# Attention layer of a graph network: maxima stored feature-major, only denominators turned back, another order on TensorE, the maximum's column copied by ScalarE

## The chip, the cores and the metric

One core of one Trainium2 chip runs the whole kernel. The metric is the time of one execution on the device in microseconds (us), the median of several runs. The profile is one execution taken by the hardware profiler. PE is TensorE, with PEld its weight loads; DVE is VectorE; ACT is ScalarE; POOL is GpSimd; SP is SyncE, which here only issues transfers.

## The reference, cut to what matters

Four graph layers follow one another on 6250 nodes and 200,000 edges sorted by destination, each with a residual and a layer norm. The change is in the fourth, an attention layer with 4 heads of 16 features:

```
xl = (x @ W_l + b_l);  xr = (x @ W_r + b_r);  e = edge_attr @ W_e       # 16 edge features
g = leaky_relu(xl[src] + xr[dst] + e, 0.2)
logits = einsum('ehc,hc->eh', g, att)
amax   = segment_max(logits, dst);   ex = exp(logits - amax[dst])
denom  = segment_sum(ex, dst);       alpha = ex / (denom[dst] + 1e-16)
out    = segment_sum(xl[src] * alpha, dst) + bias
out    = batch_norm(out) * gamma + beta;   return gelu(out + x)
```

Sums and maxima by destination are made over sorted edges: a running scan is restarted wherever the destination changes, and the row at a node's last edge is its result.

## The kernel before, in words

The edges are cut into two halves of 100,000. 512 edges of either half make a group, so there are 196 groups (n = 0 to 195, the last of 160 edges). On chip a tile is feature-major: 128 partitions are 2 halves x 64 features, and 512 columns are edges in order. The fourth layer is `edges_4`, followed by `finish_4`. The third, `edges_3`, has the same form with other steps and is not touched.

Each engine runs its own program, and semaphores join them. `each_group` takes for an engine a list of (lag, step) and runs for every tick t each step on group t - lag, in the order of the list. That written order is all that sets the order of work on an engine; nothing is reordered. The body is unrolled four times.

The steps of `edges_4` for one group:

- POOL `gather`: 8 indirect transfers fetch xl[src] into `got` (4 buffers), L1681. A buffer is free when PE has turned it (`turned_got`).
- SP `load`: 7 transfers, the destination rows (`first`), the edge features (`ea`), the marks (`mk`) and resets (`rs`), L1654 to L1657; it waits for `resets` and `owned` of four groups earlier.
- PE `gathered_rows`: turns `got` into `p_got` in four pieces; ACT `their_rows` copies that to `theirs`, L1751.
- PE `edge_inputs`: turns `first` into `p_first` and `ea` into `p_small`; ACT `edge_rows` copies the latter to `eat`, L1746.
- DVE `spread`: a scan hands each destination's row on to its edges, `own`, L1836.
- PE `add_edge_terms`: two matmuls add `eat` and `theirs` into `p_pre`, L1717 and L1719. DVE `attend` adds `own`, L1844; ACT `fifths` and DVE `leak` make the leaky relu `act_in`, L1757 and L1850.
- PE `score`: the logits into `p_logit`, L1733, then the spread resets into `p_reset`, L1735. ACT `keep_logits`, L1789.
- DVE `maximum`: copies the last column of the other `top` into column 0 of this one, L1814, then scans the maxima, L1818.
- DVE `exponents`: L1824, L1825, L1828; ACT `exps`: exp of both, L1762 and L1765, and the maxima, masked to one row of each head, into `p_reset`, L1766.
- DVE `accumulate`: scan of denominators `den`, L1858; weights times `theirs`, L1861; `mixed`, which puts denominators and maxima of a head in different rows of one tile, L1864; scan of the sums `run`, L1869.
- PE `turn_back` and `small_back`: turn `run` and `mixed` into edge-major `p_out` and `p_small` in four pieces each. ACT `to_rows` copies them to `rows`, L1772 and L1777, and `store` sends those to `t3` in DRAM, 72 columns for each edge: 64 sums, 4 denominators, 4 maxima.

The lags and the orders before are:

```
PE:  (1, gathered_rows), (0, edge_inputs), (1, add_edge_terms), (3, turn_back), (3, small_back), (1, score)
ACT: (1, their_rows), (0, edge_rows), (2, exps), (1, fifths), (3, to_rows), (3, store), (1, keep_logits)
DVE: (2, maximum), (2, exponents), (1, attend), (0, spread), (1, leak), (2, accumulate)
```

In `score` the reset matmul waits for `mixes`, so for the DVE's L1864 of the group before. `finish_4` fetches for each node the row at its last edge with 49 indirect transfers (L973), reads the row where the first half ends (`carry`), and normalizes.

Of the kernel before, what the change touches and what calls it, by code (L numbers as in the profile page):

```python
# [17 lines left out]
I32 = mybir.dt.int32  # L18
# [50 lines left out]
class Group:  # L69


    def __init__(self, it, base, unroll=UNROLL):
        self.it, self.base, self.unroll = it, base, unroll
        self.n = base if it is None else it * unroll + base
        self.row = self.n * W
        self.w = TAIL if it is None and base == NG else W
        self.p = self.w // C
        self.zero = it is None and base == 0
        self.late = it is None and base + LAG > NG
# [100 lines left out]
def build(nc, x, src, dst, ea16, ea64, ew, w0a, b0a, w0b, b0b, u1, w1a, b1a, w1b, b1b, g1, be1,  # L180
          w2a, b2a, w2b, b2b, w2g, b2g, wl, bl, wr, br, we, att, bias3, g3, be3, out):
    ctx = ExitStack()
    with ctx:
# [5 lines left out]
        t3 = dram("t3", [E, T3], F32)  # L189
        start2 = dram("start2", [E, D], F32)  # L190
# [50 lines left out]
        edges_4(nc, sb, ps, sem, ix4, ea16, marks, tabg[1], start3, prime, t3, ident, sel2, we, att)  # L241
        finish_4(nc, sb, ps, sem, X, order[0], t3, valid, bias3, g3, be3, out)
# [1365 lines left out]
def edges_4(nc, sb, ps, sem, ix, ea16, marks, tabg, start, prime, t3, ident, sel2, we, att):  # L1608
# [5 lines left out]
    with Stage(nc) as c:  # L1614
        WE, AT = sb(c, "WE", [2 * ED, P]), sb(c, "AT", [P, P])
        AV = sb(c, "AV", [P, 1])
        onesr, second = sb(c, "onesr", [P, R]), sb(c, "second", [P, R])
        for_top, for_den = sb(c, "for_top", [P, 1]), sb(c, "for_den", [P, 1])
# [5 lines left out]
        own, theirs, fifth, act_in, logit, expo, decay, run, den, mixed = (  # L1624
            [sb(c, f"{n}{i}", [P, W]) for i in range(2)] for n in ("own", "theirs", "fifth", "act_in", "logit", "expo", "decay", "run", "den", "mixed"))
# [8 lines left out]
        stored = [sem(c, f"stored{i}") for i in range(2)]  # L1634
        (resets, turned_first, turned_ea, turned_got, featured, gotten, summed_ea, owned, added, leaked, scored,
         logits, fifthed, carried, maxed, lefts, shifted, falls, grown, decayed, topped, weighted, summed, dens, mixes, rowed, smalls, drained, drained_small) = (
            sem(c, n) for n in ("resets", "turned_first", "turned_ea", "turned_got", "featured", "gotten", "summed_ea",
                                "owned", "added", "leaked", "scored", "logits", "fifthed", "carried", "maxed", "lefts", "shifted", "falls", "grown",
                                "decayed", "topped", "weighted", "summed", "dens", "mixes", "rowed", "smalls", "drained", "drained_small"))
        with nc.Block() as block:  # L1640
            @block.sync
            def _(sp):
# [16 lines left out]
                each_group(sp, (0, load))  # L1659

            @block.gpsimd
            def _(pool):
                nc.gpsimd.memset(onesr[:, :], 1.0).then_inc(made, 1)
                nc.gpsimd.memset(blocks[0][:, :], 1.0).then_inc(made, 1)
                pool.wait_ge(made, 2)

                nc.gpsimd.affine_select(out=second[:, :], in_=onesr[:, :], compare_op=ALU.is_equal, fill=0.0, base=-1,
                                        pattern=[[-HC, R]], channel_multiplier=1).then_inc(made, 1)
# [3 lines left out]
                pool.wait_ge(made, 4)  # L1672
# [15 lines left out]
            def _(pe):  # L1688
# [23 lines left out]
                def add_edge_terms(g):  # L1712
# [6 lines left out]
                    nc.tensor.matmul(p_pre[:, 0:g.w], ident[:, :], theirs[s][:, 0:g.w], start=False, stop=True).then_inc(summed_ea, 1)  # L1719

                def small_back(g):

                    pe.wait_ge(mixes, g.n + 1)
                    if not g.late:
                        pe.wait_ge(featured, g.n + LAG + 1)
                    else:
                        pe.wait_ge(drained_small, g.n)
                    turn_to_edges(nc, p_small[:, :].rearrange("p (c q) -> p c q", c=C), mixed[g.slot(2)], g, ident).then_inc(smalls, 1)

                def score(g):  # L1730
# [3 lines left out]
                    wait_from(pe, mixes, g.n)  # L1734
                    nc.tensor.matmul(p_reset[:, 0:g.w], sel2[:, :], rs[g.slot(AHEAD)][:, 0:g.w], start=True, stop=True).then_inc(resets, 1)  # L1735

                each_group(pe, (1, gathered_rows), (0, edge_inputs), (1, add_edge_terms), (3, turn_back), (3, small_back), (1, score))

            @block.scalar
            def _(act):  # L1740
                act.wait_ge(zeroed, 3)

# [5 lines left out]
                def their_rows(g):  # L1748
                    act.wait_ge(turned_got, g.n + 1)
                    wait_from(act, weighted, g.n - 1)  # L1750
                    nc.scalar.activation(by_place(theirs[g.slot(2)], g), by_block(p_got, g), ACT.Copy).then_inc(gotten, 1)  # L1751
# [7 lines left out]
                def exps(g):  # L1759
                    s = g.slot(2)  # L1760
                    act.wait_ge(shifted, g.n + 1)
                    nc.scalar.activation(p_logit[s][:, 0:g.w], p_logit[s][:, 0:g.w], ACT.Exp).then_inc(grown, 1)  # L1762
                    act.wait_ge(falls, g.n + 1)
                    wait_from(act, summed, g.n - 1)
                    nc.scalar.activation(decay[s][:, 0:g.w], expo[s][:, 0:g.w], ACT.Exp).then_inc(decayed, 1)  # L1765
                    nc.scalar.activation(p_reset[:, 0:g.w], top[s][:, 1:1 + g.w], ACT.Identity, scale=for_top[:, 0:1]).then_inc(topped, 1)  # L1766

                def to_rows(g):
# [7 lines left out]
                    for q in range(2):  # L1776
                        ins = nc.scalar.activation(rows[s][0:g.p, :, :, D + q * HEADS:D + (q + 1) * HEADS].rearrange("p h c f -> p c h f"),  # L1777
                                                   small[:, :, :, :, q], ACT.Copy)
                    ins.then_inc(drained_small, 1)
# [11 lines left out]
                each_group(act, (1, their_rows), (0, edge_rows), (2, exps), (1, fifths), (3, to_rows), (3, store), (1, keep_logits))  # L1791
# [4 lines left out]
            def _(dve):  # L1796
                nc.vector.memset(WE[:, :], 0.0).then_inc(zeroed, 1)
                dve.wait_ge(weights_in, 64)
                dve.wait_ge(made, 5)
                nc.vector.tensor_scalar(AT[:, :], blocks[2][:, :], AV[:, 0:1], None, ALU.mult).then_inc(zeroed, 1)  # L1800

                nc.vector.tensor_reduce(for_top[:, :], second[:, :], AX.X, ALU.add).then_inc(zeroed, 1)
                dve.wait_ge(zeroed, 3)
                nc.vector.tensor_scalar(for_den[:, :], for_top[:, :], -1.0, 1.0, ALU.mult, ALU.add).then_inc(zeroed, 1)
                dve.wait_ge(zeroed, 4)

                def maximum(g):
                    s = g.slot(2)
                    wait_from(dve, topped, g.n - 1)
                    if g.zero:  # L1810
                        nc.vector.memset(top[s][:, 0:1], NEG).then_inc(carried, 1)
                    else:
                        dve.wait_ge(maxed, g.n)
                        nc.vector.tensor_copy(top[s][:, 0:1], top[1 - s][:, W:W + 1]).then_inc(carried, 1)  # L1814
                    dve.wait_ge(carried, g.n + 1)
                    dve.wait_ge(logits, g.n + 1)
                    dve.wait_ge(resets, g.n + 1)
                    nc.vector.tensor_tensor_scan(top[s][:, 1:1 + g.w], p_reset[:, 0:g.w], logit[s][:, 0:g.w], top[s][:, 0:1], ALU.add, ALU.max).then_inc(maxed, 1)  # L1818

                def exponents(g):  # L1820
# [3 lines left out]
                    nc.vector.tensor_tensor(p_logit[s][:, 0:g.w], p_logit[s][:, 0:g.w], top[s][:, 1:1 + g.w], ALU.subtract).then_inc(shifted, 1)  # L1824
                    nc.vector.tensor_tensor(p_reset[:, 0:g.w], top[s][:, 0:g.w], p_reset[:, 0:g.w], ALU.add).then_inc(lefts, 1)  # L1825
# [26 lines left out]
                def accumulate(g):  # L1852
# [4 lines left out]
                    wait_from(dve, mixes, g.n - 1)  # L1857
# [3 lines left out]
                    nc.vector.tensor_tensor(p_logit[s][:, 0:g.w], theirs[s][:, 0:g.w], p_logit[s][:, 0:g.w], ALU.mult).then_inc(weighted, 1)  # L1861
                    dve.wait_ge(topped, g.n + 1)
                    wait_from(dve, smalls, g.n - 1)
# [164 lines left out]
```

## Time and profile before

| | |
|---|---|
| median of 3 runs | 5972.57 us (5963.78 to 5984.49) |
| the profiled execution, its own time | 5978.15 us |
| its span, first to last instruction | 5976.4 us |
| busy over the span | PE 65%, DVE 65%, POOL 59%, ACT 31% |
| gathers of `edges_3` issued | 1344.4 to 3303.6 us |
| gathers of `edges_4` issued | 3468.7 to 5756.5 us |
| first DVE instruction of `finish_4` | 5811.2 us |

The profile's own time is 0.1% above the median. A share over the whole span mixes stages with different limits, so the stage of `edges_4`, some 2340 us long, is to be read by itself.

### The profile page before, as it was taken

The page shows a single profiled execution, that of the slowest core. Times are in us where ns is not written, and L with a number is a line of the kernel's source. Part 1 is how long each engine was busy: PE and PEld are TensorE (multiplying, and loading weights), DVE is VectorE, ACT ScalarE, POOL GpSimd, SP SyncE. Part 2 cuts the span into 40 slices and gives each one's busy share as a digit, 9 for nine tenths or more (in the row PEclk, how much of TensorE's full clock was granted, in tenths as well). Part 3 has the DMA queues.
Part 4 walks back from the last instruction along what each step waited for, and adds up shares of the span by engine and source line. Part 5 has one row for each costly group of instructions (what it writes and reads, how often), then busy time and mean ns, then how long its engine had stood idle before and what let it go on. Part 6 is the DMA issues. An engine that isn't in the chain of part 4 may idle for free. (4 is left out here: it accounts for less than half of the span.)

```text
span 5976.4 us, 57806 instructions
## 1 busy us (share of the span) xinstructions
PE 3875.9 (65%) x12134; PEld 2170.3 (36%) x12134; DVE 3858.3 (65%) x4586; ACT 1848.3 (31%) x3478; POOL 3534.9 (59%) x3662
## 2 busy tenths in 40 slices
PE   3556669765555555555555358778877887777860
PEld 2334446432333333333333224444444444444430
DVE  9988887653333333333333457887788778888775
ACT  1233335461111111111111123443344334444330
POOL 5440025337777777777777676666666666666632
PEclk7666667776666666666666556665677666666665
DMA  8666569715444444444444234343344334334420
GB/s 188 218 190 203 177 168 272 120 35 127 116 118 118 118 118 119 118 119 118 119 118 107 52 76 88 87 87 83 84 88 88 83 85 86 87 86 88 85 58 21
DMA packets 1372199, 674.80 MB, mean 113 GB/s; under 512 B 1049375, under 2 KB 1252761, under 8 KB 1371141
## 3 DMA queue, kind: packets, MB, share of 16 engines
q1 hardware_dynamic: 1095862, 338.24, 24.3%
q0 software_dynamic: 116848, 124.33, 11.6%
q10 hardware_dynamic: 159390, 211.24, 10.1%
q14 instruction: 76, 0.61, 0.0%
q8 instruction: 23, 0.38, 0.0%
HBM read 344.06 MB, written 329.35 MB: 113 GB/s over the span
## 5 line engine op out<-in xcount | busy, mean ns | idle before, releaser
L1681 POOL DMA_INDIRECT got<-tabg,ix x1568 | 1479.7, 944 | 809.2 <-issue 425.6
L1489 POOL DMA_INDIRECT got<-tabg,ix x1568 | 1482.5, 945 | 487.4 <-issue 477.6
L1587 DVE TENSOR_TENSOR_SCAN own<-mk,own,p_first 128x512 f32<-128x512 bf16 x195 | 248.8, 1276 | 1010.4 <-PE p_first L169 1005.9
L176 PEld LDWEIGHTS p_out<-ident,run 128*128 128x128 f32 (+1 forms) x3136 | 597.5, 220 | 600.2 <-issue 542.5
L1509 PE MATMUL p_inter<-hid,W 128*128 128x512 f32 x392 | 394.2, 1109 | 568.0 <-DVE run L1595 568.0
L176 PE MATMUL p_out<-ident,run 128*128 128x128 f32 (+1 forms) x3136 | 717.2, 383 | 65.2 <-DVE run L490 48.2
L1541 ACT ACTIVATE gate<-p_gate,BF 128x512 f32<-128x512 f32 x196 | 134.5, 686 | 992.3 <-PE p_gate L1511 991.8
L1733 PE MATMUL p_logit<-act_in,AT 128*128 128x512 f32 x392 | 273.5, 786 | 238.1 <-DVE act_in L1850 238.1
L1844 DVE TENSOR_TENSOR p_pre<-own,p_pre 128x512 f32<-128x512 f32 x196 | 136.1, 694 | 439.8 <-PE p_pre L1719 439.8
L169 PE MATMUL p_first<-ident,first 128*128 128x128 f32 x1568 | 367.3, 381 | 66.7 <-DMA rs<-marks 61.3
L605 ACT ACTIVATE rows<-p_out 128x512 f32<-128x512 f32 x392 | 229.5, 597 | 531.0 <-PE p_out L176 509.0
L490 DVE TENSOR_TENSOR_SCAN run<-p_mk,run,feat 128x512 f32<-128x512 f32 x302 | 370.2, 1267 | 36.1 <-ACT feat L598 29.1
L1511 PE MATMUL p_gate<-hid,WF 128*128 128x512 f32 x392 | 363.6, 1031 | 0.0
L1717 PE MATMUL p_pre<-eat,WE 32*128 32x512 f32 x392 | 350.8, 988 | 0.0
L1719 PE MATMUL p_pre<-theirs,ident 128*128 128x512 f32 x392 | 337.2, 956 | 0.0
L561 PE MATMUL p_mk<-mk,sel 2*128 2x512 bf16 x304 | 137.1, 546 | 301.8 <-DVE run L490 301.8
L169 PEld LDWEIGHTS p_first<-ident,first 128*128 128x128 f32 x1568 | 305.4, 210 | 70.2 <-issue 65.5
L1556 ACT ACTIVATE hid<-pre,B 128x512 f32<-128x512 f32 x196 | 141.1, 720 | 593.8 <-DVE pre L1603 593.8
L1509 PEld LDWEIGHTS p_inter<-hid,W 128*128 128x128 f32 x392 | 95.2, 302 | 613.2 <-issue 545.1
L169 PE MATMUL p_got<-ident,got 128*128 128x128 f32 (+1 forms) x784 | 143.0, 310 | 261.5 <-DMA got<-tabg,ix 261.4
L1735 PE MATMUL p_reset<-rs,sel 2*128 2x512 bf16 x196 | 109.3, 557 | 229.6 <-DVE mixed L1864 229.6
L1818 DVE TENSOR_TENSOR_SCAN top<-p_reset,top,logit 128x512 f32<-128x512 f32 x196 | 250.9, 1280 | 9.8 <-ACT logit L1789 2.8
(333 smaller groups left out, 7300.1 us busy)
## 6 DMA issues: line engine op xcount, KB each, us to landing
t<-rows ACTq DMA_DIRECT2D x195, 512.0 KB
first<-start SPq DMA_DIRECT2D x780, 128.0 KB
t<-rows ACTq DMA_DIRECT2D x195, 288.0 KB
got<-tabg,ix POOLq DMA_INDIRECT x3136
start<-zeros SPq DMA_DIRECT2D x100, 500.0 KB
ea<-in_ea_dram SPq DMA_DIRECT2D x390, 128.0 KB
mk<-marks SPq DMA_DIRECT2D x780, 64.0 KB
start<-zeros SPq DMA_DIRECT2D x195, 256.0 KB
```

The costliest lines, as they stand in the source:

```text
L169: mm = nc.tensor.transpose(by_place(bank, g)[:, :, cc], by_edges[0:g.p, cc, :, :].rearrange("p h f -> p (h f)"), ident[0:g.p, 0:g.p])
L176: mm = nc.tensor.transpose(bank[0:g.p, cc, :], by_place(t, g)[:, :, cc], ident[:, :])
L490: nc.vector.tensor_tensor_scan(run[kind][s][:, 0:g.w], banks[kind][:, 0:g.w], feat[s][:, 0:g.w], initial, op0, op1).then_inc(scanned[kind], 1)
L1489: nc.gpsimd.indirect_dma_start(got[s][0:g.p, cc, h, :], None, tabg, bass.IndirectOffsetOnAxis(ap=ix[0:g.p, g.n, h, cc:cc + 1], axis=0)).th ...
L1509: nc.tensor.matmul(p_inter[s][:, 0:g.w], W2[:, :], hid[s][:, 0:g.w], start=True, stop=True).then_inc(mixed, 1)
L1511: nc.tensor.matmul(p_gate[:, 0:g.w], WF[:, :], hid[s][:, 0:g.w], start=True, stop=True).then_inc(scored, 1)
L1587: nc.vector.tensor_tensor_scan(own[s][:, 0:g.w], mk[m][:, 0:g.w], p_first[s][:, 0:g.w], prime[:, 0:1] if g.zero else own[1 - s][:, W - 1:W ...
L1681: nc.gpsimd.indirect_dma_start(got[s][0:g.p, cc, h, :], None, tabg, bass.IndirectOffsetOnAxis(ap=ix[0:g.p, g.n, h, cc:cc + 1], axis=0)).th ...
L1717: nc.tensor.matmul(p_pre[:, 0:g.w], WE[:, :], eat[s][:, 0:g.w], start=True, stop=False)
L1719: nc.tensor.matmul(p_pre[:, 0:g.w], ident[:, :], theirs[s][:, 0:g.w], start=False, stop=True).then_inc(summed_ea, 1)
L1733: nc.tensor.matmul(p_logit[g.slot(2)][:, 0:g.w], AT[:, :], act_in[g.slot(2)][:, 0:g.w], start=True, stop=True).then_inc(scored, 1)
L1818: nc.vector.tensor_tensor_scan(top[s][:, 1:1 + g.w], p_reset[:, 0:g.w], logit[s][:, 0:g.w], top[s][:, 0:1], ALU.add, ALU.max).then_inc(max ...
```

## The change

- The maxima leave the way back to edges. SP stores rows 0, 16, ..., 112 of `top` (one for each half and head) into a new DRAM table `tops`, 8 runs of 2 KB for a group (`store_top`, lag 5). `maximum` waits until the store of two groups earlier has landed.
- L1864 (`mixed`) and L1766 go. `den` itself is turned back. `rows` keeps its 72 columns, the last four zero; one ACT copy for the denominators instead of two.
- `maximum` takes its start value from the other `top`; its copy L1814 is done by ACT inside `exps`, for `exponents`.
- The reset matmul waits for `falls` (L1828 of the group before) instead of `mixes`.
- `theirs` has 4 buffers instead of 2. `edge_inputs` is split into `first_rows` and `edge_rows`. PE and ACT have other lags and orders.
- `finish_4` works out the last edge, fetches its four maxima from `tops` in one indirect transfer ahead of the 49, and turns and broadcasts them on PE. A second small transfer brings the maxima where the first half ends.

The diff, cut to its core:

```diff
+        tops = dram("tops", [2 * HEADS, H], F32)
...
+        theirs = [sb(c, f"theirs{i}", [P, W]) for i in range(4)]
...
+                def store_top(g):
+                    s = g.slot(2)
+                    sp.wait_ge(maxed, g.n + 1)
+                    sp.dma_start(tops[:, ds(snapped(sp, g.row), g.w)], top[s][0:P:HC, 1:1 + g.w]).then_inc(tops_out[s], 16)
+                each_group(sp, (0, load), (5, store_top))
...
-                def edge_inputs(g):
+                def first_rows(g):
                     s = g.slot(AHEAD)
                     pe.wait_ge(first_in[s], 80 * g.turn(AHEAD) + 80)
                     wait_from(pe, owned, g.n)
                     turn_in_order(nc, p_first, first[s], g, ident).then_inc(turned_first, 1)
+                def edge_rows(g):
+                    s = g.slot(AHEAD)
                     wait_from(pe, featured, g.n)
-                    wait_from(pe, drained_small, g.n - LAG)
+                    wait_from(pe, drained_small, g.n - 2)
...
                 def small_back(g):
-                    pe.wait_ge(mixes, g.n + 1)
-                    if not g.late:
-                        pe.wait_ge(featured, g.n + LAG + 1)
+                    pe.wait_ge(dens, g.n + 1)
+                    if g.it is not None or g.base + 2 <= NG:
+                        pe.wait_ge(featured, g.n + 3)
...
                 def score(g):
...
-                    wait_from(pe, mixes, g.n)
+                    wait_from(pe, falls, g.n)
...
-                each_group(pe, (1, gathered_rows), (0, edge_inputs), (1, add_edge_terms), (3, turn_back), (3, small_back), (1, score))
+                each_group(pe, (2, score), (1, add_edge_terms), (0, first_rows), (3, turn_back), (3, small_back), (0, gathered_rows), (0, edge_rows))
...
                 def their_rows(g):
-                    wait_from(act, weighted, g.n - 1)
+                    wait_from(act, weighted, g.n - 3)
...
                 def exps(g):
                     nc.scalar.activation(p_logit[s][:, 0:g.w], p_logit[s][:, 0:g.w], ACT.Exp).then_inc(grown, 1)
+                    if not g.last:
+                        wait_from(act, lefts, g.n)
+                        nc.scalar.activation(top[1 - s][:, 0:1], top[s][:, W:W + 1], ACT.Copy).then_inc(carried, 1)
...
-                    nc.scalar.activation(p_reset[:, 0:g.w], top[s][:, 1:1 + g.w], ACT.Identity, scale=for_top[:, 0:1]).then_inc(topped, 1)
...
-                each_group(act, (1, their_rows), (0, edge_rows), (2, exps), (1, fifths), (3, to_rows), (3, store), (1, keep_logits))
+                each_group(act, (2, exps), (1, fifths), (3, to_rows), (3, store), (0, their_rows), (0, edge_rows), (1, keep_logits))
...
                 def maximum(g):
-                    wait_from(dve, topped, g.n - 1)
...
-                        nc.vector.tensor_copy(top[s][:, 0:1], top[1 - s][:, W:W + 1]).then_inc(carried, 1)
-                    dve.wait_ge(carried, g.n + 1)
+                    wait_from(dve, tops_out[s], 16 * g.turn(2))
+                    wait_from(dve, maxed, g.n)
+                    wait_from(dve, decayed, g.n - 1)
                     dve.wait_ge(logits, g.n + 1)
                     dve.wait_ge(resets, g.n + 1)
-                    nc.vector.tensor_tensor_scan(top[s][:, 1:1 + g.w], p_reset[:, 0:g.w], logit[s][:, 0:g.w], top[s][:, 0:1], ALU.add, ALU.max).then_inc(maxed, 1)
+                    nc.vector.tensor_tensor_scan(top[s][:, 1:1 + g.w], p_reset[:, 0:g.w], logit[s][:, 0:g.w],
+                                                 NEG if g.zero else top[1 - s][:, W:W + 1], ALU.add, ALU.max).then_inc(maxed, 1)
...
-                    nc.vector.scalar_tensor_tensor(out=mixed[s][:, 0:g.w], in0=den[s][:, 0:g.w], scalar=for_den[:, 0:1], in1=p_reset[:, 0:g.w],
-                                                   op0=ALU.mult, op1=ALU.add).then_inc(mixes, 1)
...
             def _(pool):
-                pool.wait_ge(cleared, 1)
+                nc.gpsimd.iota(base[:, :], pattern=[[0, 1]], base=(HEADS - 1) * H, channel_multiplier=H).then_inc(based, 1)
+                pool.wait_ge(placed, 1)
+                pool.wait_ge(cleared, 2)
+                nc.gpsimd.indirect_dma_start(final[:, :], None, tops.rearrange("a r -> (a r)").rearrange("(n o) -> n o", o=1),
+                                             bass.IndirectOffsetOnAxis(ap=where[:, :], axis=0),
+                                             bounds_check=2 * HEADS * H - 1, oob_is_err=False).then_inc(final_in, 16)
                 gather_rows(pool, nc, rows, T3, t3, info["last"], rows_in)
...
+                link(nc.vector.tensor_copy(ends[:, :], info["last"][:, :]))
+                link(nc.vector.tensor_tensor(counted[:, :], ends[:, :], info["span"][:, :], ALU.mult))
+                link(nc.vector.tensor_reduce(spanned[:, :], counted[:, :], AX.X, ALU.add))
+                dve.wait_ge(based, 1)
+                link(nc.vector.tensor_copy(basef[:, :], base[:, :]))
+                dve.wait_ge(turned, 1)
+                link(nc.vector.tensor_tensor(place[:, :], basef[:, :], p_where[0:HEADS, :], ALU.add))
+                nc.vector.tensor_copy(where[:, :], place[:, :]).then_inc(placed, 1)
```

## Rows read from the trace of the kernel before

**Rows 1.** Stretches of edges_3 and edges_4: busy us (x count), PEclk, DMA share, GB/s.
```profile
2000.00:2500.00 500.00, 289.89 (x800) 156.82 (x800) 195.17 (x201) 98.89 (x150) 378.10 (x401) 0.68 0.48 118
4500.00:5000.00 500.00, 407.31 (x1126) 210.87 (x1124) 394.22 (x499) 198.11 (x419) 314.31 (x334) 0.63 0.40 85
```

**Rows 2.** The gathers by source line: count, ns min/median/max, first and last start; idle reasons.
```profile
L1681 POOL DMA_INDIRECT got<-tabg,ix x1568: 905/944/1027, 3468.7 to 5756.5; - x196
...
  PE p_got L162: 383.6, 178
...
L1489 POOL DMA_INDIRECT got<-tabg,ix x1568: 899/945/975, 1344.4 to 3303.6; - x196
```

**Rows 3.** Who waited for whom, 3600 to 5700 us: us in total, times, longest.
```profile
DVE p_pre L1844 <- PE p_pre L1719: 392.1, 176, 3.0
```

**Rows 4.** Timeline of one group of edges_4: start us, us, engine, line, operation.
```profile
4611.60 1.13 PE L1733 MATMUL p_logit<-act_in,AT 128*128 128x512 f32 x2 [1.67 <-DVE act_in L1850]
...
4612.76 0.60 ACT L1789 ACTIVATE logit<-p_logit 128x512 f32<-128x512 f32 x1 [1.68 <-PE p_logit L1733]
...
4614.17 0.60 PE L1735 MATMUL p_reset<-rs,sel 2*128 2x512 bf16 x1 [1.45 <-DVE mixed L1864]
...
4615.22 0.13 DVE L1814 COPY top<-top 128x1 f32<-128x1 f32 x1
4615.38 1.28 DVE L1818 TENSOR_TENSOR_SCAN top<-p_reset,top,logit 128x512 f32<-128x512 f32 x1
...
4618.03 0.69 DVE L1828 TENSOR_TENSOR expo<-p_reset,top 128x512 f32<-128x512 f32 x1
...
4619.29 0.30 SPq L1657 DMA_DIRECT2D rs<-marks  x1
...
4621.64 0.70 DVE L1844 TENSOR_TENSOR p_pre<-own,p_pre 128x512 f32<-128x512 f32 x1 [2.92 <-PE p_pre L1719]
...
4624.01 1.27 DVE L1858 TENSOR_TENSOR_SCAN den<-decay,den,p_logit 128x512 f32<-128x512 f32 x1
```

**Rows 5.** The masked mixing by line, 3600 to 5700 us: busy us, mean ns.
```profile
L1864 DVE SCALAR_TENSOR_TENSOR mixed<-den,for_den,p_reset 128x512 f32<-128x512 f32 x177 | 131.2, 741 | 0.0
```

**Rows 6.** PE timeline of a group wholly at the lower clock.
```profile
4707.91 2.08 PE L1733 MATMUL p_logit<-act_in,AT 128*128 128x512 f32 x2 [0.92 <-DVE act_in L1850]
4710.48 0.60 PE L1735 MATMUL p_reset<-rs,sel 2*128 2x512 bf16 x1 [0.49 <-DVE mixed L1864]
...
4718.49 1.06 PE L176 MATMUL p_small<-ident,mixed 128*128 128x128 f32 x4
```

**Rows 7.** PE timeline of pieces at the upper clock.
```profile
4606.80 1.12 PE L1717 MATMUL p_pre<-eat,WE 32*128 32x512 f32 x2
...
4609.28 0.64 PE L176 MATMUL p_small<-ident,mixed 128*128 128x128 f32 x4
...
4626.72 0.38 PE L1735 MATMUL p_reset<-rs,sel 2*128 2x512 bf16 x1 [1.45 <-DVE mixed L1864]
```

**Rows 8.** Short stretches of edges_4, columns as in rows 1.
```profile
4603.50:4606.50 3.00, 2.99 (x13) 2.25 (x13) 2.93 (x4) 0.60 (x1) 1.68 (x2) 0.50 0.32 67
...
4610.00:4613.00 3.00, 1.13 (x2) 0.30 (x2) 2.97 (x4) 1.32 (x5) 2.09 (x4) 1.00 0.40 120
4614.00:4617.00 3.00, 2.83 (x12) 2.21 (x13) 2.93 (x5) 0.60 (x1) 1.86 (x2) 0.50 0.30 66
```

**Rows 9.** The view of transfers: a store of edges_3, its KB, us from issue to landing.
```profile
t<-rows ACTq DMA_DIRECT2D x195, 256.0 KB, 2.2
```

**Rows 10.** Timeline where the gathers of edges_3 end, and where edges_4 ends.
```profile
3305.97 0.65 PE L169 MATMUL p_got<-ident,got 40*128 40x40 f32 x4 [0.90 <-DMA got<-tabg,ix]
...
5791.70 0.64 PE L162 MATMUL p_got<-ident,got 40*128 40x40 f32 x4
...
5811.16 3.00 DVE L1922 MEMSET rows<- 128x3528 f32 x1 [6.16 <-PEq L65]
...
5815.01 1.03 POOL L973 DMA_INDIRECT rows<-t,last  x1 [57.57 <-DVE rows L1922]
```

More of the change, by code:

```diff
@@ L78, in __init__ @@
         self.zero = it is None and base == 0
+        self.last = it is None and base == NG
         self.late = it is None and base + LAG > NG
@@ L240, in build @@
         node_chain(nc, sb, ps, sem, X, order[1], order[0], dst, nid, ident, prime, t2, (wl, wr), (bl, br), tabg[1], tabo[1], start3)
[L241 to L242 removed]
+        edges_4(nc, sb, ps, sem, ix4, ea16, marks, tabg[1], start3, prime, t3, tops, ident, sel2, we, att)
+        finish_4(nc, sb, ps, sem, X, order[0], t3, tops, ident, valid, bias3, g3, be3, out)
 def node_rows(flat):
@@ L1623, in edges_4 @@
         rs = [sb(c, f"rs{i}", [2, W], BF16) for i in range(AHEAD)]
-        own, theirs, fifth, act_in, logit, expo, decay, run, den, mixed = (
-            [sb(c, f"{n}{i}", [P, W]) for i in range(2)] for n in ("own", "theirs", "fifth", "act_in", "logit", "expo", "decay", "run", "den", "mixed"))
+        own, fifth, act_in, logit, expo, decay, run, den = (
+            [sb(c, f"{n}{i}", [P, W]) for i in range(2)] for n in ("own", "fifth", "act_in", "logit", "expo", "decay", "run", "den"))
+        theirs = [sb(c, f"theirs{i}", [P, W]) for i in range(4)]
         eat = [sb(c, f"eat{i}", [2 * ED, W]) for i in range(2)]
@@ L1775, in to_rows @@
                     small = p_small[0:g.p, :].rearrange("p (c h a f) -> p c h a f", h=2, a=HEADS, f=HC)
[L1776 to L1779, printed above, removed]
+                    nc.scalar.activation(rows[s][0:g.p, :, :, D:D + HEADS].rearrange("p h c f -> p c h f"),
+                                         small[:, :, :, :, 0], ACT.Copy).then_inc(drained_small, 1)
                 def store(g):
@@ L1872, in _, with finish_4 @@
                 each_group(dve, (2, maximum), (2, exponents), (1, attend), (0, spread), (1, leak), (2, accumulate))
-def finish_4(nc, sb, ps, sem, X, info, t3, valid, bias3, g3, be3, out):
+def finish_4(nc, sb, ps, sem, X, info, t3, tops, ident, valid, bias3, g3, be3, out):
     with Stage(nc) as c:
@@ L1892, in _ @@
             def _(sp):
-                sp.dma_start(carry[:, :], t3[H - 1:H, :].to_broadcast((P, T3))).then_inc(small_in, 16)
+                sp.dma_start(carry[:, 0:D + HEADS], t3[H - 1:H, 0:D + HEADS].to_broadcast((P, D + HEADS))).then_inc(small_in, 16)
+                with nc.allow_non_contiguous_dma(reason="the heads' maxima where the first half ends"):
+                    sp.dma_start(carry[:, D + HEADS:T3], tops[0:HEADS, H - 1:H].rearrange("a o -> o a").to_broadcast((P, HEADS))).then_inc(small_in, 16)
                 for t, w in ((BI, bias3), (GA, g3), (BE, be3)):
@@ L1975, in _ @@
             def _(pe):
+                pe.wait_ge(chain, 4)
+                nc.tensor.matmul(p_where[:, :], ones[:, :], spanned[:, :], start=True, stop=True).then_inc(turned, 1)
+                pe.wait_ge(final_in, 16)
+                nc.tensor.matmul(p_final[:, :], final[:, 0:1].to_broadcast((HEADS, P)), ident[0:HEADS, 0:HEADS], start=True, stop=True).then_inc(turned, 1)
                 for n in range(2):
```

67 lines of the change are left out of this document (33 added, 34 removed).

## The prediction

> **What bounds the kernel now.** I read the page's slices first: the last two fifths of the span belong to the fourth layer, and there neither PE nor DVE is full. Then I set that stage beside the third layer, whose gathers are the same [rows 1]. In 500 us POOL issues 401 gathers in the third layer and 334 in the fourth; at 8 for a group that is 50.1 and 41.75 groups, so 9.98 us and 11.98 us for a group. The view by source line says the same for the whole stages [rows 2]: 1567 steps in 1959.2 us are 1.250 us for a gather and 10.0 us for a group, against 2287.8 us, 11.7 us for a group. A gather itself takes as long in both, 944 and 945 ns. In the fourth layer POOL waits 383.6 us for PE to have turned an old buffer. So POOL could go at 10.0 us for a group and is held back.
>
> By what, the waits and one group's timeline show. DVE waits 392.1 us in 177 groups, 2.2 us each, for one thing only, the sum `p_pre` [rows 3]. PE in turn stands still before the reset matmul L1735 until DVE has made `mixed` [rows 4]. Behind that matmul PE has everything else in its order: the turns of `got`, `first` and `ea` and then both matmuls of `p_pre`, for which DVE waits at L1844, 2.92 us in this group. The two engines take turns in a ring: DVE's accumulation, PE's turns and edge terms, DVE's attend, spread and leak. Neither is full by itself: for a group DVE is busy 394.22 / 41.75 = 9.44 us and PE 407.31 / 41.75 = 9.76 us [rows 1], and the group takes 12.
>
> **The change part by part.** *DVE.* L1864 goes, 0.74 us [rows 5], and the copy L1814, 0.13 us [rows 4]. That leaves 9.44 - 0.87 = 8.57 us for a group. The copy goes to ACT as a 128x1 instruction; ACT loses L1766 and one small copy and is the least busy engine by far (198.11 us in 500 [rows 1]), so it costs nothing there. If that cover were gone, the subtraction L1825 would be late by the copy, some 0.2 us.
>
> *PE.* The number of matmuls stays. What changes is their place: turns of `got` and `ea` now stand at the end of the tick, where PE has been idle, and `p_pre` follows the score directly. The reset matmul waits for L1828 of the group before, which is done long before the leak that releases the score; that wait costs nothing. How long PE needs depends on its clock. A group wholly at the lower level (0.50, 1.2 GHz) runs from 4707.91 to 4718.49 + 1.06, 11.64 us, of which 0.49 are the wait at the reset: 11.15 us of work [rows 6]. At the upper level (1.00, 2.4 GHz) both pairs of `p_pre` and two turns take 4606.80 to 4609.92, 3.12 us; the reset takes 0.38 [rows 7], the score 1.13 [rows 4], and three more turns at 0.64 take 1.92 [rows 7]: 6.55 us. PE keeps to 10.0 us a group if no more than (10.0 - 6.55) / 4.6 = 0.75 of its work falls to the lower level. Before, by 9.76 us, it is 0.70. Which way will that move? From 4603.5 to 4606.5 PE worked without a break and was at 0.50; afterwards the same pieces run at the upper level, and it still is 1.00 from 4610 to 4613, where PE worked only 1.13 us; after that idle stretch it is back at 0.50 [rows 7, 8]. Unbroken work raises the clock and idle stretches drop it. The new order joins score, reset and `p_pre` with the turns into one unbroken run and leaves one gap instead of two. I take the share at the lower level as no higher than before, so 8.5 to 9.8 us for a group; 6.6 and 11.15 stay as ends.
>
> The Trainium skill has a rule that speaks against this (TensorE: Matmul & The Clock Gate, Part 4: PE-mode transpose): transposes do not count as TensorE work for the clock. By it the five blocks of turns that now stand together would let the clock fall in every group. This trace does not agree: in the stretch at 4603.5 the 13 matmuls are the reset and turns, and the clock rose behind them. What it would cost is bounded by the all-lower case below.
>
> *The ring.* At the lower clock, from the start of the score: score 2.08 [rows 6], logits 0.60, maximum to the end of L1828 4615.38 to 4618.72 = 3.34, attend to the next accumulation 2.37 [rows 4]: 8.4 us, with hand-overs some 8.7. By the other branch, score 2.08, reset 0.60, two pairs for `p_pre` at the score's 2.08, then 2.37: 9.2. A third runs over ACT, whose order now puts the copies of `got` and `ea` behind the store: up to `p_pre` the same 6.8, attend 0.70, then ACT's leaky copy and `rows` (128x512 like the logits, 0.60 each), the denominators' copy (some 0.2, an estimate from their 32 columns) and the turn of `ea` 1.06: 10.0. All at the worse clock throughout; with any part at the upper level all three are under 10.0. So what ends last is POOL's own pace, as in the third layer. DVE, 86% busy then, doesn't slow POOL: the gather's 944 ns are the same at 39% and at 79% DVE busy [rows 1, 2]. DMA, at 0.48 in the third layer, is not full there either.
>
> *SP and the store of maxima.* SP gets an eighth transfer for a group, some 0.5 us like its others. The store of group g-2 is sent behind the load of group g+3, and that begins once the resets of g-1 are made. From the reset's start (4614.17) to the end of the last load's issue (4619.59) are 5.4 us [rows 4]; with 0.5 for its own issue and 2.2 to land, the nearest row for a store to DRAM [rows 9], it is down 8.1 us after that reset. The maximum of g needs it when its logits are copied, 10.0 + 0.6 us after the same reset. Slack 2.5 us, so the wait costs nothing. From below a landing can't cost less than nothing; from above it is the rival below. The next load, queued behind it on SP, has three groups of time.
>
> *The sum, against the profiled execution's own 5978.15 us.* The last gather starts at 3468.7 + 1959.2 = 5427.9; where the third layer's gathers end, `p_got` is worked on 2.4 us after the last start [rows 2, 10], so 5430.3 instead of 5791.70 [rows 10]: -361.4. The tail from there was 19.5 us to `finish_4`; now a turn, a whole score and a logit copy (2.3 to 3.3 us) stand ahead, and about 1.0 of `mixed` falls out: +2. In `finish_4` POOL's 49 gathers waited for a memset of 3.00 us, and everything after waits for them; now they also wait for seven short DVE instructions, a matmul and a gather of 1.03 + 0.3 us [rows 10]. No row shows that chain; with 0.13 us for a link (the copy) and a matmul of 0.6 it would be 1.5, with 0.35 for each 3.0. Together with the gather 2.8 to 4.4, I take +3.2. The second small load and the turn of the maxima lie under the 49 gathers, over 60 us. The start is unchanged. Sum -356: 5978.15 - 356 = 5622; the profile's own time is 5.6 us above the median, so against that it is 5617. I say 5619.
>
> **The rivals.**
>
> *PE becomes the bound.* If the clock stays low in every group, the pace is 11.15 us instead of 10.0: 196 x 1.15 = 225 us back, 5844. Halfway, with a few groups over 10.0 that the four `got` buffers can't smooth, 5730. For it: 9.76 us is close to 10.0, and the in-order PE now waits for gathers with a score queued behind. Against it: the clock rises behind unbroken work [rows 7, 8], and a PE that is always busy is just that. By the rule of the Trainium skill named above this is the case that comes about. Chance 0.12.
>
> *The maximum waits for its store* (the one that can end slower). The pace is then 5.4 + 0.5 + landing - 0.6 us. It decides from a landing of 4.7 us; each further us costs 196 us, and beyond 6.6 us the kernel is slower than before. At 7.0 the pace is 12.3 against 2342 / 196 = 11.95 us before: +69, 6042. For it: 8 runs of 2 KB behind 7 loads in the same queue, a shape the trace doesn't show. Against it: 2.2 us for 256 KB. Chance 0.06, of which 0.02 still faster, 0.01 unchanged, 0.03 slower.
>
> *Nothing changes,* because the ring only shifts: PE waits for the leak, DVE for `p_pre`, at the old pace. For it: all of DVE's order is kept. Against it: the four blocks that stood between `mixed` and `p_pre` are reduced to the reset. 5973, chance 0.02.
>
> **How the numbers follow.** The pace of the gathers has 0.80, and the predicted time is its 5619; its own range is 5605 to 5650. The range to hold 8 in 10 reaches into the case of PE: 5603 to 5720. A measurement of this kernel tells about 0.3% from no change, 18 us. Faster by more: 0.80 + 0.12 + 0.02 = 0.94; within it 0.01 + 0.02 = 0.03; slower 0.03.
>
> **What the changed kernel's profile would show.** Right: gathers 1.25 us apart from first to last and ending near 5429 us, hardly a wait of POOL for `p_got`; PE's longest wait at the turns of `got`, on the gathers' landing; DVE busy near 8.6 us for a group; `finish_4` near 5452. PE the bound: a granted clock at 0.50 to 0.55 in the stage, PE over 95% busy, POOL still waiting for PE. Store: DVE idle on a DMA before the scan that is L1818 now. Wrong altogether: a gather that takes longer when DVE and PE are denser, or ACT's ring closing later than reckoned, with PE waiting for the denominators' copy before it turns `ea`.

## The result, and the profile after

| | before | changed |
|---|---|---|
| median | 5968.17 us (4 runs, 5957.86 to 5984.49) | 5607.35 us (4 runs, 5603.70 to 5610.51) |
| the profiled execution, its own time | 5978.15 us | 5607.81 us |
| its span | 5976.4 us | 5606.1 us |
| gathers of `edges_4` issued | 3468.7 to 5756.5 us | 3453.4 to 5413.9 us |
| first DVE instruction of `finish_4` | 5811.2 us | 5437.10 us |

The ratio is 0.9393, with a 95% interval of 0.937 to 0.9416: 6.1% faster. 5619 us was predicted, with 5603 to 5720 as the range.

The same stretches as in [rows 1], in the changed kernel:

```profile
2000.00:2500.00 500.00, 285.62 (x800) 154.66 (x800) 195.43 (x200) 98.61 (x150) 378.22 (x400) 0.69 0.47 118
4500.00:5000.00 500.00, 377.22 (x1350) 208.38 (x1350) 441.43 (x500) 211.87 (x450) 378.02 (x401) 0.78 0.47 104
```

The third layer is as it was. In the fourth POOL now issues 401 gathers in 500 us, 9.98 us for a group of 8. For a group DVE is busy 441.43 / 50.1 = 8.81 us and PE 377.22 / 50.1 = 7.53 us, at a granted clock of 0.78 instead of 0.63.

The gathers of the fourth layer by source line, for [rows 2]:

```profile
L1685 POOL DMA_INDIRECT got<-tabg,ix x1568: 907/947/981, 3453.4 to 5413.9; - x196
...
  issue: 478.0, 1568
```

1567 steps in 1960.5 us are 1.251 us each. POOL sits idle 0.30 us ahead of each for its own issue and for nothing else; the 383.6 us for `p_got` are gone. The gather takes as long as before, 947 ns against 944.

Who waited for whom from 3600 to 5350 us, for [rows 3]: us in total, times, longest.

```profile
PE p_got L163 <- DMA got<-tabg,ix: 434.7, 153, 5.0
POOL got L1685 <- issue: 426.6, 1399, 0.3
...
DVE top L1819 <- ACT logit L1794: 167.5, 117, 3.6
...
DVE p_pre L1847 <- PE p_pre L1726: 10.4, 55, 0.4
```

DVE's wait for `p_pre` has fallen from 392.1 us (176 groups) to 10.4 us (175 groups lie in this stretch). In its place PE waits for gathers that haven't landed: 434.7 us, 2.8 us in each of 153 groups. That is how the profile looks when POOL sets the pace and everything behind it has time to spare.

One group in the timeline, for [rows 4] and [rows 7]:

```profile
4598.65 0.39 PE L1742 MATMUL p_reset<-rs,sel 2*128 2x512 bf16 x1
...
4598.87 1.02 PE L1724 MATMUL p_pre<-eat,WE 32*128 32x512 f32 x2
...
4599.82 1.13 PE L1726 MATMUL p_pre<-theirs,ident 128*128 128x512 f32 x2
...
4602.83 0.69 DVE L1847 TENSOR_TENSOR p_pre<-own,p_pre 128x512 f32<-128x512 f32 x1
...
4604.11 0.69 SPq L1664 DMA_DIRECT2D tops<-top  x1
...
4605.82 1.12 PE L163 MATMUL p_got<-ident,got 128*128 128x128 f32 x4 [3.48 <-DMA got<-tabg,ix]
```

The reset no longer waits, `p_pre` follows it at once and is whole at 4600.95, 1.9 us before DVE adds to it. PE's one idle stretch is ahead of the turns of `got`.

**Where the 370.3 us went** (profiled executions). The first gather of `edges_4` starts 15.3 us earlier, in stages that the change doesn't touch; no step foresaw that, and it isn't explained. The third layer's gathers already start 16.6 us earlier (1327.8 instead of 1344.4). Executions of the kernel before differ among themselves by up to 26.6 us, and its profiled one is 10 us above their median, so part of this may be the scatter of single executions. From the first to the last gather: 1960.5 instead of 2287.8 us, -327.3. From the last gather to `finish_4`: 23.2 instead of 54.7 us, -31.5, because the backlog of groups behind the gathers is gone. From there to the end of the span: 169.0 instead of 165.2 us, +3.8. Together -370.3.

The start of `finish_4`, for [rows 10]:

```profile
5437.10 3.00 DVE L1933 MEMSET rows<- 128x3528 f32 x1 [6.36 <-PEq L65]
...
5442.99 0.97 POOL L1908 DMA_INDIRECT final<-tops,where  x1 [6.56 <-DVE where L1943]
5444.26 1.04 POOL L975 DMA_INDIRECT rows<-t,last  x1 [0.30 <-issue]
```

The 49 gathers begin 7.16 us after the memset's start, before 3.85 us: +3.3. The rest of the 3.8 lies behind them.

### The profile page after: what moved, and what is told of

It reads as the page before. It is cut to its first block and busy times, and to the rows that moved or that the text cites. A ratio compares the mean times of both kernels' runs of the same rounds, so it can differ in the third digit from the quotient of the medians.

```text
span 5606.1 us, 58135 instructions
## 1 busy us (share of the span) xinstructions
PE 3461.3 (62%) x12138; PEld 1991.0 (36%) x12138; DVE 3723.9 (66%) x4203; ACT 1748.2 (31%) x3281; POOL 3545.3 (63%) x3662
## 3 DMA queue, kind: packets, MB, share of 16 engines
q10 hardware_dynamic: 159390, 211.24, 10.8%
## 5 line engine op out<-in xcount | busy, mean ns | idle before, releaser
L177 PE MATMUL p_out<-ident,run 128*128 128x128 f32 (+1 forms) x3136 | 673.5, 363 | 80.7 <-DVE run L492 58.9
L177 PEld LDWEIGHTS p_out<-ident,run 128*128 128x128 f32 (+1 forms) x3136 | 558.7, 217 | 436.4 <-issue 355.1
L163 PE MATMUL p_got<-ident,got 128*128 128x128 f32 (+1 forms) x784 | 178.9, 370 | 492.2 <-DMA got<-tabg,ix 491.9
L170 PE MATMUL p_first<-ident,first 128*128 128x128 f32 x1568 | 305.9, 331 | 66.6 <-DMA rs<-marks 61.3
L170 PEld LDWEIGHTS p_first<-ident,first 128*128 128x128 f32 x1568 | 256.9, 180 | 211.4 <-issue 205.3
L170 PE MATMUL p_got<-ident,got 128*128 128x128 f32 (+1 forms) x784 | 142.4, 309 | 269.7 <-DMA got<-tabg,ix 269.7
L1740 PE MATMUL p_logit<-act_in,AT 128*128 128x512 f32 x392 | 305.2, 875 | 1.9 <-DVE act_in L1853 1.9
L163 PEld LDWEIGHTS p_got<-ident,got 128*128 128x128 f32 (+1 forms) x784 | 115.7, 183 | 529.4 <-DMA got<-tabg,ix 529.0
L1726 PE MATMUL p_pre<-theirs,ident 128*128 128x512 f32 x392 | 279.2, 801 | 0.0
L1767 ACT ACTIVATE p_logit<-p_logit 128x512 f32<-128x512 f32 x196 | 113.8, 580 | 461.4 <-DVE p_logit L1826 453.6
```

Source lines behind the costliest of these rows:

```text
L163: mm = nc.tensor.transpose(bank[0:q, cc * P:cc * P + g.p], by_edges[0:g.p, cc, :, :].rearrange("p h f -> p (h f)"), ident[0:g.p, 0:g.p])
L170: mm = nc.tensor.transpose(by_place(bank, g)[:, :, cc], by_edges[0:g.p, cc, :, :].rearrange("p h f -> p (h f)"), ident[0:g.p, 0:g.p])
L177: mm = nc.tensor.transpose(bank[0:g.p, cc, :], by_place(t, g)[:, :, cc], ident[:, :])
L1726: nc.tensor.matmul(p_pre[:, 0:g.w], ident[:, :], theirs[g.slot(4)][:, 0:g.w], start=False, stop=True).then_inc(summed_ea, 1)
L1740: nc.tensor.matmul(p_logit[g.slot(2)][:, 0:g.w], AT[:, :], act_in[g.slot(2)][:, 0:g.w], start=True, stop=True).then_inc(scored, 1)
```

## The experiments

Each kernel was timed beside the one before on the same chip; the ratio is to that. The theory behind the prediction (A) says that the new place of the turns on PE frees the ring. The rival (B) says that taking `mixed` and its wait away is enough for the gathers' pace, whatever the order.

One thing has to be known for reading the numbers. Eleven of the twelve runs below fell on chips on which the unchanged kernel took 6645 to 6698 us instead of 5968. The stretches of [rows 1] on such a chip, for the changed kernel run again there (E0):

```profile
2000.00:2500.00 500.00, 230.13 (x686) 132.69 (x685) 163.16 (x169) 83.96 (x128) 321.45 (x341) 0.69 0.40 101
4500.00:5000.00 500.00, 347.93 (x1113) 180.62 (x1113) 365.81 (x411) 176.45 (x372) 311.94 (x331) 0.70 0.39 86
```

The untouched third layer goes at 341 gathers in 500 us there instead of 400. That layer in the timeline of the same run:

```profile
2004.67 0.95 POOL L1491 DMA_INDIRECT got<-tabg,ix  x1 [0.30 <-issue]
2005.37 2.97 SPq L1477 DMA_DIRECT2D first<-start  x2
...
2009.10 0.60 ACT L1549 ACTIVATE rows<-p_out 128x512 f32<-128x512 f32 x1 [6.67 <-remote]
...
2009.45 0.95 POOL L1491 DMA_INDIRECT got<-tabg,ix  x1 [3.83 <-DMA wsum<-wall]
```

Each gather takes what it took, but about once in a group POOL stands still for 2 to 4 us (the 0.30 us for its issue included). In this stretch nothing starts on SP, ACT, DVE or POOL from the end of SP's issues at 2008.34 to 2009.05. The releaser that the view names for POOL is a transfer of a stage long past, so it names none. What holds them up was not found; it holds for both kernels, so ratios from such chips are compared only with ratios from such chips.

**E0: the changed kernel again.** No edit.

> The changed kernel again, beside the three that undo one part of it. Both theories: 0.939 of the kernel before, some 5607 us; gathers of the attention layer 1.250 us apart, 1960 us from first to last.

6575.10 us (6568.25 to 6577.01), before 6645.03: ratio 0.9891, 0.9857 to 0.9925. The gathers go at 12.1 us for a group. Both theories had said 0.939 and gathers 1.250 us apart, and on this chip neither comes out. The change is worth 1.1% where the engines are held up and 6.1% where they are not. Here the store of maxima is waited for, by the waits from 4100 to 5700 us:

```profile
DVE top L1819 <- DMA tops<-top: 168.2, 55, 4.2
```

**E1 and E6: the changed kernel with the orders of before.** Two waits of PE on `p_small` (before the turns of `ea` and of `den`) go back to their old form with the order; the diff shows the orders alone.

```diff
-each_group(pe, (2, score), (1, add_edge_terms), (0, first_rows), (3, turn_back), (3, small_back), (0, gathered_rows), (0, edge_rows))
+each_group(pe, (1, gathered_rows), (0, first_rows), (0, edge_rows), (1, add_edge_terms), (3, turn_back), (3, small_back), (1, score))
-each_group(act, (2, exps), (1, fifths), (3, to_rows), (3, store), (0, their_rows), (0, edge_rows), (1, keep_logits))
+each_group(act, (1, their_rows), (0, edge_rows), (2, exps), (1, fifths), (3, to_rows), (3, store), (1, keep_logits))
```

> The changed kernel with the orders of TensorE and ScalarE as before (all else stays: no mixed tile, maxima stored by SP, reset waits for falls, four buffers). Theory A (the order is what frees the ring of TensorE and VectorE): the three blocks of turns stand between score and p_pre again, so the ring holds; it loses only the wait for mixed, 0.5 to 1.5 us of a group. Pace 10.3 to 10.9 us a group, so 5665 to 5785 us, with TensorE's unbroken run perhaps at the better end; POOL still waits for p_got. Rival B (the removed mixed and its wait were what held the ring): pace 10.0, 5607 us, no difference from the changed kernel.

> The changed kernel with the orders of TensorE and ScalarE as before, once more on another chip, because on the first one POOL is held up for some 2 us in each group of both kernels. Theory A as before, sharpened by the first run (order worth 2.8% there): pace 10.3 to 10.9 us, ratio to the kernel before 0.948 to 0.969. Rival B: 0.939.

E1: 6750.82 us, before 6645.03, ratio 1.0173 (1.0108 to 1.0239). E6: 6766.12 us, before 6698.41, ratio 1.0089 (1.0072 to 1.0107). On the held-up chips the changed kernel with the old orders is slower than the one before, and E1 is 2.7% slower than E0 on the same chip. Neither theory had this. The waits of E1 from 4100 to 5700 us:

```profile
POOL got L1685 <- PE p_got L163: 213.6, 30, 10.8
DVE p_pre L1847 <- DMA wsum<-wall: 198.0, 19, 13.5
```

In this list DVE waits 10.4 us on average in 19 groups (the transfer named is one of a stage long past), and POOL stands behind a full set of buffers in 30 groups. E0's list has no wait longer than 7.1 us in its first twelve lines. Why the waits are longer with the old orders was not found. So neither run could tell theory from rival; that took a chip without the stops.

**E10: the same kernel, on a chip without the stops.**

> The changed kernel with the orders of TensorE and ScalarE as before, a third time. On a chip without hold-ups theory A says a pace of 10.3 to 10.9 us and a ratio of 0.948 to 0.969, rival B 0.939. On a chip with hold-ups 1.009 to 1.017 as in the two runs before.

5609.98 us (5607.14 to 5619.06), before 5960.52: ratio 0.9412 (0.939 to 0.9433). The changed kernel has 0.9393 (0.937 to 0.9416); the intervals overlap. Its stretch of the fourth layer, and its waits from 3600 to 5350 us:

```profile
4500.00:5000.00 500.00, 404.41 (x1342) 217.41 (x1343) 436.13 (x498) 208.92 (x447) 378.07 (x400) 0.76 0.47 104
```

```profile
POOL got L1685 <- issue: 426.9, 1401, 0.3
...
PE p_logit L1740 <- DVE act_in L1853: 314.1, 175, 2.9
...
DVE p_pre L1847 <- PE p_pre L1726: 196.4, 129, 3.1
```

POOL goes at 10.0 us for a group and waits for nothing. The ring is still there, with the turns between score and `p_pre`: DVE waits 196.4 us for `p_pre`, half of the 392.1 of [rows 3]. But on average it closes within 10 us. PE's part of it in the timeline:

```profile
4599.82 1.13 PE L1740 MATMUL p_logit<-act_in,AT 128*128 128x512 f32 x2 [1.67 <-DVE act_in L1853]
4600.88 0.38 PE L1742 MATMUL p_reset<-rs,sel 2*128 2x512 bf16 x1
4602.00 1.00 PE L163 MATMUL p_got<-ident,got 128*128 128x128 f32 x4 [0.74 <-DMA got<-tabg,ix]
...
4606.14 1.13 PE L1726 MATMUL p_pre<-theirs,ident 128*128 128x512 f32 x2
```

From the score's start to the reset's are 1.06 us, in [rows 4] 2.57. What is gone is the wait for `mixed` and, on DVE, `mixed` itself. The theory of the order falls for such a chip; the rival holds. E10 also keeps four `theirs`, the copy on ACT and the stores of maxima, and it doesn't part these from `mixed`. The buffers are a weak rival: in the kernel before, ACT's copy into `theirs` waits for PE's turn (178 groups in the view of [rows 3]), and no line of that view has it waiting for a free buffer.

The ring's length goes with PE's clock, and the averages hide that. Scores and second matmuls of `p_pre` in the kernel before, to be set beside the score at 4611.60 in [rows 4]:

```profile
4600.94 1.13 PE L1733 MATMUL p_logit<-act_in,AT 128*128 128x512 f32 x2 [1.67 <-DVE act_in L1850]
...
4607.85 1.12 PE L1719 MATMUL p_pre<-theirs,ident 128*128 128x512 f32 x2
...
4619.45 2.08 PE L1719 MATMUL p_pre<-theirs,ident 128*128 128x512 f32 x2
...
4624.15 1.12 PE L1733 MATMUL p_logit<-act_in,AT 128*128 128x512 f32 x2 [0.92 <-DVE act_in L1850]
```

With `p_pre` at the upper level it is 10.66 us from score to score, with `p_pre` at the lower 12.55. In E10:

```profile
4621.16 1.13 PE L1740 MATMUL p_logit<-act_in,AT 128*128 128x512 f32 x2 [1.33 <-DVE act_in L1853]
...
4629.99 2.07 PE L1740 MATMUL p_logit<-act_in,AT 128*128 128x512 f32 x2 [2.87 <-DVE act_in L1853]
...
4641.98 2.08 PE L1740 MATMUL p_logit<-act_in,AT 128*128 128x512 f32 x2 [0.92 <-DVE act_in L1853]
```

These are 8.83 us with PE at the upper level and 11.99 at the lower. Counted over the timeline from 3600 to 5350 us, the kernel before has no group under 10.5 us, 56 groups near 10.8 and 92 near 12.5; E10 has 72 near 9.0 and 28 near 11.9. So E10's ring is longer than POOL's 10.0 us in part of its groups. It is the average that stays within 10.0, and POOL, with four `got` buffers, never waits. Both things are needed for it: with `mixed` not even the groups at the upper level were under 10, and without it the groups at the lower level still are not. The granted clock in the stretch is 0.76 instead of 0.63; why it rose with the old order in place was not tested.

**E2, E7, E9 and E11: the order alone.** The kernel before with the new orders of PE and ACT, `edge_inputs` split and four `theirs`; `mixed`, the masked copy and the DVE's copy stay, and no maxima are stored. The diff is cut to the orders.

```diff
-each_group(pe, (1, gathered_rows), (0, edge_inputs), (1, add_edge_terms), (3, turn_back), (3, small_back), (1, score))
+each_group(pe, (2, score), (1, add_edge_terms), (0, first_rows), (3, turn_back), (3, small_back), (0, gathered_rows), (0, edge_rows))
-each_group(act, (1, their_rows), (0, edge_rows), (2, exps), (1, fifths), (3, to_rows), (3, store), (1, keep_logits))
+each_group(act, (2, exps), (1, fifths), (3, to_rows), (3, store), (0, their_rows), (0, edge_rows), (1, keep_logits))
...
```

> The kernel before with the new lags and orders of TensorE and ScalarE, the split of the edge inputs and four buffers for theirs, and nothing else: mixed, the masked copy and the 128x1 copy stay, the reset waits for mixed, maxima go back with the denominators. Theory A: the ring runs score, wait for mixed (2.6 us after the leak), reset, p_pre 2.1 to 4.1, attend to leak 2.4, so 8 to 9.9 us; gathers set the pace at 10.0 and the time is within 15 us of the changed kernel, 5595 to 5625. Rival B: the wait for mixed holds it at the old pace of 11.95, 5950 to 5985 us.

> The kernel before with the new orders and the four buffers alone, once more. Theory A: ratio 0.937 to 0.943, the whole of the change. Rival B: 1.0.

> The kernel before with the new orders and four buffers alone, a third time, in the hope of a chip on which the engines are not held up between instructions. There theory A says the whole of the change: ratio 0.937 to 0.943, pace of the gathers 10.0 us. On a chip with hold-ups: 0.975 to 0.99 as in the two runs before.

> The kernel before with the new orders and four buffers alone, a fourth time, right after the old order without mixed gave 0.9412 on a chip without hold-ups, against theory A's 0.948 to 0.969. Theory A in its new form (either part alone opens the ring far enough for the gathers to set the pace): 0.937 to 0.943, gathers at 10.0 us a group. Theory B (only taking mixed and its wait away opens it): the reset still waits 2.6 us after the leak, pace 11 to 12 us, ratio 0.97 to 1.0.

| | this, us | before, us | ratio (95%) |
|---|---|---|---|
| E2 | 6580.21 | 6645.03 | 0.9903 (0.9868 to 0.9938) |
| E7 | 6537.77 | 6698.41 | 0.9753 (0.9731 to 0.9774) |
| E9 | 6601.20 | 6669.69 | 0.9896 (0.9866 to 0.9927) |
| E11 | 6590.82 | 6655.52 | 0.9887 (0.9853 to 0.9921) |

All four fell on held-up chips. There the order alone gives what the whole change gives, 0.9903 against E0's 0.9891 on one chip. A's 0.937 to 0.943 came out in none, B's 1.0 in none of the first three. E11 lies in B's later range of 0.97 to 1.0, but on such chips E0, the whole change, does too, so it decides nothing. Whether the order alone would also bring the 10.0 us where nothing is held up stays open: no such run exists. DVE keeps `mixed` there and is busy 392.89 us for 329 gathers in E2's stretch from 4500 to 5000 us, 9.55 us for a group, which leaves little room under 10.0.

**E3 and E8: six gathers for a group instead of eight.** The fourth piece of `got` is set to zero once and not fetched, and PE waits for six landings instead of eight; the diff shows the loop alone.

```diff
-for cc in range(C):
+for cc in range(3):
```

> The changed kernel with six of a group's eight gathers: the rows of the fourth piece are left out and stay zero, so the output is not the reference's. The gathers' own pace falls to 7.5 us a group. Theory A (only the gathers set the pace at 10.0): the next limit shows, VectorE's 8.6 us with cracks or the ring, 8.9 to 9.3 us a group, so 5390 to 5470 us. Rival (TensorE at its lower clock or another wait already holds some 10.0 by itself): 5580 to 5610 us.

> The changed kernel with six of eight gathers (the fourth piece stays zero, so the output is not the reference's), once more. Theory A: pace 8.9 to 9.3 us, ratio 0.903 to 0.917. Rival: 10.0, ratio 0.935 to 0.94.

E3: 6102.80 us, ratio 0.9158 (0.9132 to 0.9184), inside theory A's 0.903 to 0.917; E8: 6029.68 us, 0.8999 (0.8984 to 0.9014), just below it. Both ranges were meant for a chip without stops. The gathers of E3 by source line:

```profile
L1689 POOL DMA_INDIRECT got<-tabg,ix x1176: 909/947/983, 3994.0 to 5883.2; - x196
```

1175 steps in 1889.2 us are 9.65 us for six, 2.5 less than the 12.1 of E0: the price of two gathers of 1.25 us, and in E8 9.45, 2.6 less than the 12.04 of E7 (the order alone) on its chip. On these chips POOL, its gathers and its stops together, sets the pace. But not by much: POOL now waits for PE again, 209.9 us in 74 groups, and DVE is busy 453.55 of 500 us (4500 to 5000).

**E4: the store of maxima one group later.**

```diff
-each_group(sp, (0, load), (5, store_top))
+each_group(sp, (0, load), (6, store_top))
```

> The changed kernel with the store of the maxima one tick later in SP's program (lag 6 instead of 5). The maximum of a group then waits for a store that is sent only behind the load which that same group's resets release. Theory A (the store costs nothing now because it has some 2 us of slack): the wait becomes a part of the ring, 5.4 us of load issues, 0.7 of its own, 2.2 to 2.6 to land, then 5.7 from the maximum to the leak and 1.2 to 2.2 for the score: 15.2 to 16.6 us a group, 6620 to 6900 us. Rival (SP runs so far ahead that the store is never late): no difference, 5607 us.

7284.53 us, before 6651.07: ratio 1.0941 (1.0914 to 1.0968), 15.7 us for a group, inside the 15.2 to 16.6 that theory A gave. Its waits from 4100 to 5700 us:

```profile
DVE top L1819 <- DMA tops<-top: 697.0, 100, 8.0
POOL got L1685 <- PE p_got L163: 631.6, 101, 10.4
```

DVE waits 7 us in every group for the store, and POOL behind it. The wait that the change adds is a real one. With lag 5 it is never the last on the quiet chip; one place later it costs 3.6 us a group more than E0.

**E5: two buffers for `theirs` instead of four.**

```diff
-theirs = [sb(c, f"theirs{i}", [P, W]) for i in range(4)]
+theirs = [sb(c, f"theirs{i}", [P, W]) for i in range(2)]
```

> The changed kernel with two buffers for theirs instead of four, so ScalarE's copy of the gathered rows waits until the weighting of two groups before is done, some 2 us after the leak. Theory A: that delays the copies of the edge features and of the logits by up to 1 us, the ring grows to 9 to 9.7 us and stays under the gathers' 10.0: no difference, 5600 to 5620 us. Rival (ScalarE's order closes the ring): pace 10.3, some 5665 us.

6576.83 us, ratio 0.99 (0.9866 to 0.9934), E0 on the same chip 0.9891. Both theories spoke of a chip without stops; on this one the extra buffers bring nothing.

No version beats the changed kernel with certainty. E10's old orders are level with it on a quiet chip and lose 2.7% where engines are held up, which speaks for the new ones.

## Why the prediction was right, point by point

- **The bound before** (a ring between DVE and PE, with POOL's own 10.0 us as the floor): right. The gathers' stretch was predicted at 1959.2 us and took 1960.5; POOL waits for its own issue alone, and E3 and E8 take off two gathers' time. (DVE's wait for `p_pre` stands 176 times in [rows 3], not 177.)
- **The reason given for the ring's end** was too narrow. The prediction put it on the turns that leave the place between score and `p_pre`. E10 puts them back and keeps 10.0 us for a group: without `mixed`, its wait at the reset and the DVE's copy the old ring also closes in time on average. The gathers' floor ends the time with the old orders as with the new ones, so that the time came out doesn't speak for the reason. The order adds slack (DVE's wait for `p_pre` 10.4 us instead of 196.4) that a quiet chip doesn't need.
- **DVE** at 8.57 us for a group: 8.81 measured, 0.24 too low; it hides under 10.0.
- **PE** at 8.5 to 9.8 us was the worst-sized term: 7.53. The sum kept the share of work at the lower level where it had been, 0.70; by the prediction's own two ends, 6.55 and 11.15, the measured work means (7.53 - 6.55) / 4.6 = 0.21. That the share would not rise was right, and the reason given isn't shown: E10 has the old order, PE as busy as before (404.41 us in 500, 407.31 before) and a clock of 0.76 instead of 0.63, close to the new order's 0.78. Nor does unbroken work raise the clock by itself. Stretches of the changed kernel, with columns as in [rows 8]:

```profile
4593.70:4597.40 3.70, 3.70 (x19) 3.48 (x18) 3.53 (x4) 2.21 (x5) 2.79 (x4) 0.50 0.55 94
4598.00:4602.00 4.00, 4.00 (x18) 2.04 (x17) 3.93 (x5) 1.45 (x3) 2.85 (x4) 1.00 0.47 108
4602.00:4605.00 3.00, 0.34 (x3) 0.15 (x2) 2.96 (x5) 2.10 (x6) 2.33 (x3) 0.91 0.62 119
4606.00:4613.50 7.50, 7.50 (x15) 3.05 (x16) 5.71 (x7) 2.47 (x5) 5.67 (x7) 0.50 0.36 85
```

  After the idle stretch that ends at 4605.82 the clock is at 0.50, and it was at 1.00 before. It then stays at 0.50 through 7.50 us in which PE never stops. The rule of the Trainium skill (TensorE: Matmul & The Clock Gate, Part 4: PE-mode transpose) would have kept it from rising behind the five joined blocks of turns. The 19 matmuls from 4593.70 to 4597.40 all belong to those five blocks, at 0.50, and behind them the clock is at 1.00, so the trace doesn't agree with it.
- **The store of maxima** with 2.5 us of slack: not once waited for in the profile after. Its issue takes 0.69 us instead of 0.5; when it lands the profile doesn't give. E4 shows the rival's mechanism at its full price, and E0 shows it starting (168.2 us in 55 groups) where SP is held up: the slack is real and small.
- **The tail**: +2 predicted, from the first turn of the last `got` (5416.23) to `finish_4` 20.9 us against 19.5 ([rows 10]), +1.4.
- **`finish_4`**: +3.2 predicted, from 2.8 to 4.4; +3.3 where the 49 gathers begin and +3.8 at the end.
- **The sum**: the stage from its first gather and `finish_4` together, -356 predicted, -355.0 measured. What makes 5607 of 5619 is the 15.3 us ahead of the stage, which no step covered. By the medians, 5968.17 and 5607.35, the whole difference is 360.8 us.
- **The rivals**: PE did not become the bound, the store did not, and the ring did not only shift.

## What to carry to other kernels

When two engines wait for each other in a ring and a third has a floor of its own, reckon the ring against that floor and not against zero: a part of the change that brings its average under the floor earns all of the gain, and the rest is slack. If the ring's length follows the clock, reckon it at either level and not by the mean alone. To learn which part earned it, undo one at a time, on a chip where an untouched stage keeps its pace; compare that stage first in every run. A semaphore wait on a store that shares its issuing queue with loads is priced by its place in that queue: one place cost 3.6 us a group here (E4 against E0).

## What the runs showed of the hardware that was not expected

- On several chips engines stood still for 2 to 4 us about once in 12 us, in layers that the change doesn't touch as in the fourth; the one before took 6645 to 6698 us there instead of 5960 to 5968, with each gather as short as ever. On SP, register moves that take 29 ns and at most 38 in the quiet run last up to 1517 ns:

```profile
L1655 SPq MOVE first<-start x376: 29/29/38, 3509.1 to 5381.6; - x188
```

```profile
L1655 SPq MOVE first<-start x376: 2/29/1517, 4075.0 to 6351.4; - x188
```

  The first row is of the changed kernel on the quiet chip, the second of E0: count, ns min/median/max. Such a chip turns a gain of 6.1% into 1.1%, and another version's gain of 5.9% (E10) into a loss of 0.9 to 1.7% (E6, E1).
- An indirect gather of 128 rows takes 944 to 947 ns and 0.30 us to issue whether DVE is busy 39%, 79% or 88% of the time ([rows 1], [rows 2] and the profile after).
